# Page scatters of a mixture-of-experts kernel: each waits for the scatter two places ahead in its group of six

## The reference

```
h = silu(x @ eg_w[e].T) * (x @ eu_w[e].T)      # 128 -> 64
routed = sum over the 6 chosen e of weight_e * (h @ ed_w[e].T)
```

## Time and profile before

| | |
|---|---|
| median of 3 runs | 593.04 us (592.63 to 596.7) |
| span of the profiled execution | 792.4 us |
| mean granted TensorE clock in it | 0.675 |
| busy: PE, PE weight loads | 503.3 us, 420.8 us |
| busy: DVE, ACT, POOL | 456.1 us, 352.3 us, 389.3 us |
| stage 1 ends (first page load) | 379.52 us |
| first gather | 454.37 us |

### The profile page before, as it was taken

One profiled execution on the slowest core, in us unless ns is written; L12 is line 12 of the kernel. 1 busy time (PEld: TensorE's weight loads), 2 busy tenths in 40 slices (PEclk: granted clock), 3 DMA queues, 4 the chain that ended last, 5 costly groups with the idle time before them and its releaser, 6 DMA issues.

```text
span 792.4 us, 12061 instructions
## 1 busy us (share of the span) xinstructions
PE 503.3 (64%) x3204; PEld 420.8 (53%) x3204; DVE 456.1 (58%) x2264; ACT 352.3 (44%) x962; POOL 389.3 (49%) x425
## 2 busy tenths in 40 slices
PE   3767555766555574632359956788688889777700
PEld 2445334444334343311359856778688789777700
DVE  6587556667555576656233624576776756346532
ACT  3564433344443343322215934466666766246400
POOL 2006445654455655556650055454554545555574
PEclk9885555555555555555568976899988876897555
DMA  7532123322123332223425533455455555654421
GB/s 195 194 113 94 62 100 107 104 100 98 47 80 107 107 100 98 95 78 129 124 81 134 148 94 95 106 138 151 126 145 137 151 137 146 160 153 107 113 70 47
DMA packets 98708, 90.60 MB, mean 114 GB/s; under 512 B 10576, under 2 KB 85456, under 8 KB 98640
## 3 DMA queue, kind: packets, MB, share of 16 engines
q1 hardware_dynamic: 85232, 64.26, 27.5%
q0 software_dynamic: 12288, 25.29, 11.3%
q10 hardware_dynamic: 1120, 0.28, 0.2%
HBM read 41.32 MB, written 48.46 MB: 113 GB/s over the span
## 4 chain that ended last, share of the span: by engine, by line
PE 30%; another core or an unknown queue 17%; issue 16%; ACT 14%; POOL 11%; DVE 9%; ACTq 2%; DMA 0%; POOLq 0%; DVEq 0%
PE bank_s L1155 14%; POOL pages L447 6%; PE bank_o L1155 4%; PE bank_q L1155 3%; PE bank_s L1151 2%; ACT d_now L511 2%; ACT p_t L533 2%; ACT pxt L511 2%; POOL empty L492 2%; ACT gu_now L511 2%; ACT k_exp L521 1%; ACT s_act L672 1%; POOL p_t L492 1%; PE bank_o L1151 1%
## 5 line engine op out<-in xcount | busy, mean ns | idle before, releaser
L1155 PE MATMUL bank_s<-pxt,gu_now 128*128 128x64 f32 x768 | 116.5, 316 | 51.6 <-ACT pxt L511 31.3
L492 POOL DMA_INDIRECT p_t<-results,place_i x96 | 91.1, 949 | 110.6 <-ACT s_act L672 72.8
L1155 PEld LDWEIGHTS bank_s<-pxt,gu_now 128*128 128x128 f32 x768 | 111.4, 231 | 58.1 <-ACT pxt L511 36.4
L492 POOL DMA_INDIRECT empty<-results,place_i x96 | 91.1, 949 | 77.2 <-issue 35.1
L1111 DVE TENSOR_TENSOR h_t<-bank_s,s_act 64x256 f32<-64x256 f32 x128 | 54.7, 427 | 113.9 <-ACT s_act L672 95.4
L447 POOL DMA_INDIRECT pages<-payload,place_i x96 | 93.0, 968 | 37.9 <-issue 27.0
L447 POOL DMA_INDIRECT pages<-payload_b,place_i x96 | 92.8, 967 | 35.8 <-issue 26.7
L437 POOL TENSOR_TENSOR rstd<-ve,minus_half 128x4 f32<-128x4 f32 (+1 forms) x21 | 18.6, 885 | 132.6 <-DVE ve L927 130.0
L672 ACT ACTIVATE s_act<-bank_s 64x512 f32<-64x512 f32 x64 | 37.8, 590 | 79.5 <-remote 36.0
L533 ACT ACTIVATE p_t<-bank_s 128x512 f32<-128x512 f32 x64 | 36.2, 598 | 67.9 <-issue 27.9
L1255 PE MATMUL bank_o<-bias_h,row_h 96*128 96x256 bf16 x16 | 6.1, 381 | 72.2 <-ACT o_t L511 70.3
(11 more groups left out here) (169 smaller groups left out, 1164.1 us busy)
## 6 DMA issues: line engine op xcount, KB each, us to landing
pg<-pages SPq DMA_DIRECT2D x64, 258.0 KB
results<-y_s SPq DMA_DIRECT2D x64, 256.0 KB
pages<-empty SPq DMA_DIRECT2D x21, 774.0 KB
w_gu<-in_expert_gu SPq DMA_DIRECT2D x16, 256.0 KB
w_d<-in_expert_d SPq DMA_DIRECT2D x31, 128.0 KB
out_x<-xb SPq DMA_DIRECT2D x16, 128.0 KB
xb<-in_x SPq DMA_DIRECT2D x3, 512.0 KB, 8.0
pages<-payload,place_i POOLq DMA_INDIRECT x96
```

The lines of the kernel that those rows point to most:

```text
L492: pool.indirect_dma_start(out=ys[n % YS_SLOTS][:, k, :], out_offset=None, in_=results[0:landed * QUAD * P, :], in_offset=bass.IndirectOffs ...
L1155: return pe.matmul(dst, w, v, start=True, stop=True)
```

## The change

Each group of six scatters gets two semaphores in place of one, used in turn by even and odd k. From the third scatter of a group on, POOL waits before it issues scatter k until scatter k-2 has landed. The waits of SP, ACT and DVE for a whole group become two waits, each for half the count. Nothing else changes; data, rows and DMAs are the same.

```
--- before.py
+++ after.py
@@ -79,6 +79,7 @@
 UPFRONT = 5
 MADE = 8
 POWER_AFTER = {}
+IN_FLIGHT = 2
 
 
 def build(nc, x, ctx_cols, wq, bq, wk, bk, wv, bv, wo, bo, gate_cols, gate_bias, expert_gu, expert_d, shared_gu, shared_d, out, pages, results):
@@ -239,7 +240,7 @@
         logit_done, sig_ready, route, chosen_ready = sem("logit_done"), sem("sig_ready"), sem("route"), sem("chosen_ready")
         ranks_done, ranks_ready, placed = sem("ranks_done"), sem("ranks_ready"), sem("placed")
         payload_x, place_ready, digits_done, packed = sem("payload_x"), sem("place_ready"), sem("digits_done"), sem("packed")
-        scattered = [[sem(f"scattered{i}_{t}") for t in range(TPB)] for i in range(2)]
+        scattered = [[[sem(f"scattered{i}_{t}_{turn}") for turn in range(IN_FLIGHT)] for t in range(TPB)] for i in range(2)]
         page_in = [sem(f"page_in{j}") for j in range(SLOTS)]
         y_out = [sem(f"y_out{j}") for j in range(SLOTS)]
         pxt_done, pxt_ready, gu_done, act_ready, h_ready = sem("pxt_done"), sem("pxt_ready"), sem("gu_done"), sem("act_ready"), sem("h_ready")
@@ -363,7 +364,8 @@
             def pages_complete(batches):
                 for i in range(2):
                     for t in range(TPB):
-                        sp.wait_ge(scattered[i][t], 16 * TOPK * ((batches - i + 1) // 2))
+                        for landed in scattered[i][t]:
+                            sp.wait_ge(landed, 16 * TOPK // IN_FLIGHT * ((batches - i + 1) // 2))
 
             def store_results(q):
                 j = q % SLOTS
@@ -443,10 +445,13 @@
 
             def scatter(n, t, first, after):
                 wait_payload(n, t)
+                landed = scattered[n % 2][t]
                 for k in range(first, after):
+                    if k >= IN_FLIGHT:
+                        pool.wait_ge(landed[k % IN_FLIGHT], 16 * (TOPK // IN_FLIGHT * (n // 2) + k // IN_FLIGHT))
                     pool.indirect_dma_start(out=pages[:, :], out_offset=bass.IndirectOffsetOnAxis(
                         ap=place_i[:, TPB * n + t, k:k + 1], axis=0), in_=payload[n % 2][:, t, k, :],
-                        in_offset=None).then_inc(scattered[n % 2][t], 16)
+                        in_offset=None).then_inc(landed[k % IN_FLIGHT], 16)
 
 
 
@@ -578,7 +583,8 @@
 
             def fill_payload(n, side, t):
                 act.wait_ge(xn2_ready, TPB * n + t + 1)
-                act.wait_ge(scattered[n % 2][t], 16 * TOPK * (n // 2))
+                for landed in scattered[n % 2][t]:
+                    act.wait_ge(landed, 16 * TOPK // IN_FLIGHT * (n // 2))
                 copy(payload[n % 2][:, t, :, 0:D], xn2[side][:, t, :].unsqueeze(1).to_broadcast([P, TOPK, D])).then_inc(payload_x, 1)
 
             def body(b):
@@ -835,7 +841,8 @@
                 chained("filled_to", dve.tensor_tensor(filled_to[:, :], ranks[:, TPB, :], fill[:, :], ALU.add))
                 chained("rank", dve.tensor_tensor(rank[:, :, :], ranks[:, 0:TPB, :], both(fill), ALU.add))
                 for t in range(TPB):
-                    dve.wait_ge(scattered[n % 2][t], 16 * TOPK * (n // 2))
+                    for landed in scattered[n % 2][t]:
+                        dve.wait_ge(landed, 16 * TOPK // IN_FLIGHT * (n // 2))
                 chained("expert", dve.tensor_copy(pay[:, :, :, EXPERT].bitcast(U32), top_at[:, :, 8 - TOPK:8]))
                 after("filled_to")
                 chained("full", dve.tensor_scalar(full[:, :], filled_to[:, :], float(U), None, ALU.is_gt))
```

## The result

The changed kernel takes 646.68 us (643.7 to 647.64, four runs) beside 593.56 us for the kernel before on the same chip (592.63 to 596.7): 1.088 times as long, interval 1.0835 to 1.0921. It is slower, as forecast, but by 53 us where the forecast had 17, and it lies outside the range that I gave, 592 to 622 us.

What follows compares the result with a forecast made beforehand. POOL's own path was taken to bound timed runs, summing to 593 us without slack; 13 bodies delayed 1.4 us beside SP's burst make 18 us, taken as 17: 610 us, forecast's own range 602 to 618, whole range 592 to 622.

Steps and rivals of the forecast that it cites:

- POOL has no slack in a timed run: Stage 1: timed runs leave no room for an idle POOL, at most 0 to 0.7 us a body.
- The sum of POOL's path: Whole run: 290.5 us to first page load, then 12.1 + 43 + 238 + 9.1, in all 593 us, the median.
- The rival in which the slack swallows the waits: Stage 1: POOL's idle time absorbs the 1.4 us a body, so 593 to 597 us; chance 0.27.
- a quiet wait is free: Scatters outside SP's burst: packets started 2.1 us after issue, 0.4 us before scatter k wants to start; no cost.
- the 2.15 us that the prediction set beside them: Quiet scatter of 66 KB: the Trainium skill's estimate, about 2.0 us plus bytes / 436 GB/s; no quiet scatter waits.
- the size of a landing beside the burst: t = 1 groups: fourth scatter lands 3.6 us after issue, sixth starts 1.4 us later; 13 x 1.4 = 18 us.
- the delay is one and not a sum of several: t = 1 groups: the fifth scatter's wait is part of the sixth's 1.4 us delay, not one more.
- More than one wait in a group: Rival: with 0.78 us releases quiet groups wait too, 13 x 2.7 = 35 us, 628 us; 0.14 with lower clock.
- The lower clock: Rival: longer POOL bodies idle PE to half clock, 626 us for five bodies, 680 for all; 0.14 shared.
- the sign that the prediction gave: If quiet groups wait as well, the wrongly sized term is the release, from landing to scatter's start, 0.28 or 0.78 us.
- Nothing became faster: Rival: fewer POOL packets beside SP's burst let it land sooner, 585 us or only 0.6 us gained; chance 0.05.
- some 20 us less of waiting for `ve`: Sign in the changed trace: POOL's wait for DVE's `ve` falls from 130.0 us by some 20 us, if half clock again.

Runs made afterwards that it cites:

- the added instruction: The kernel before with one more small POOL instruction per body, between `rstd` and the t = 1 scatters, its result unused: 610.91 us, 1.026 times before.

## Why the prediction was right in its direction and wrong in its size

**That POOL has no slack in a timed run: right.** The sum of POOL's path made 593 us, and the slack was put at 0 to 0.7 us a body. The trace without waits has its terms: first page load at 294.8 (290.5 in the sum), 51 us from there to the first gather (55), 242 us to the last gather (238), 9.1 to the end (9.1), 596.8 in all. Each is within 5 us, so the sum did not come out by luck. The slack is 0.2, by the added instruction, and the loss reaches the end whole (48 us at the first page load, at the first gather and at the end). The rival in which the slack swallows the waits, with 0.27, is refuted, and so is its basis, the 7.3 us of idle time in the trace of before.

**Why that trace showed them: my reading was wrong, and it didn't enter the sum.** I saw TensorE at half clock there and took the timed runs to have the full one. The body of the kernel without waits runs at the same clock, 0.50, with the same PE work, in 16.54 us (columns as in the earlier trace rows):

```profile
106.07:122.61 16.54, 14.00 (x84) 9.56 (x80) 14.46 (x87) 9.19 (x23) 12.62 (x14) 0.50 0.38 130
```

Most of the 7 us lay on ACT. Before, then without waits, ACT's `sig`, which waits for PE's four matmuls over `gw_t`:

```profile
102.17 1.11 PE L1155 MATMUL bank_r<-gw_t,x_all 128*128 128x64 f32 x4
...
110.23 0.28 ACT L546 ACTIVATE sig<-bank_r 128x128 f32<-128x128 f32 x1 [3.68 <-remote]
```

```profile
97.02 1.12 PE L1162 MATMUL bank_r<-gw_t,x_all 128*128 128x64 f32 x4
...
98.71 0.31 ACT L551 ACTIVATE sig<-bank_r 128x128 f32<-128x128 f32 x1
```

In the profiled execution of before ACT stood idle for the 3.68 us up to 110.23, though PE had been done since 103.3, and once more for 2.60 us before `q_t`. In the trace without waits it is nothing and 0.96 us. What held ACT up in that execution stays open.

**That a quiet wait is free: wrong, by 0.6 us a group.** I took the landing at 2.1 us from the packets. It is 2.27 to 2.39 us, and 2.54 to 2.66 with the start, just over the 2.52 us that were free, and now and then a landing is 0.8 to 1.4 us later, likely by an instruction fetch. The 2.1 us were the time until all packets had started, and the landing came 0.4 us after that; the 2.15 us that the prediction set beside them were short as well. With 14 groups that is the 8.7 us of the run with waits at t = 0.

**The step that failed: the size of a landing beside the burst.** The forecast had 13 x 1.4 = 18 us here, and it was 39.0 us, 14 x 2.8. I read the landing from the number of packets that POOL's queue had started: 131 by 103.42 us, so the fourth scatter's 32 were through the earlier trace rows. The changed trace lets one do both readings for the same scatter, the third of its group, issued at 117.43. The queue from 114.38 us, when the group begins, to 121.00 us:

```profile
q1 hardware_dynamic: 445, 1.31, 58.4%
q0 software_dynamic: 97, 0.23, 9.5%
q14 instruction: 2, 0.02, 1.3%
```

97 packets are those of three scatters, so by my method it had landed 3.6 us after its issue. But the fifth scatter, which waits for it, starts at 122.42, 0.27 us after the landing: 4.7 us after the issue. A count says how many packets have started. It does not say whose they are, nor when they land. A scatter raises its semaphore 16 times, and by the times of these events in the trace the third's came from 121.15 to 122.15, while the fourth's began at 121.57, before the last four of the third. So some parts of the fourth scatter landed before the last ones of the third. What held those up, SP's packets (58.4% of the DMA engines' time) or the 8 KB fetch that ran here from 120.68 for 0.83 us, this one scatter does not show. The semaphore is full only with the last part, and even in quiet 0.4 us after the last packet has started: of the scatter at 124.94 and the one before it, all 64 packets had started at 126.90, and the landing is at 127.34.

```profile
q0 software_dynamic: 64, 0.13, 20.9%
```

It is not this scatter alone. In the run with waits at t = 1 alone, the third scatters of all 14 such groups land 4.6 us after their issue on average (3.1 to 6.0), and the count of packets gives 3.5 for the same ones. Their first packets set out only 2.7 us after the issue, in place of 1.5 in quiet.

With the landing measured, the same working gives the right size: 4.7 + 0.27 - 2.52 = 2.4 us at the fifth scatter, beside the 2.8 measured with a small part at the others, and 14 x (2.4 + 0.6) = 42 us of 47.5; the average landing of 4.6 us gives the same to 0.1 us a body. That the delay is one and not a sum of several was right: half the waits cost 41.9 of 47.5 us. And the pair that counts is the third and fifth, and in two of the 14 bodies the fourth and sixth; I had looked at the second pair alone.

**The rivals.** "More than one wait in a group", with 0.14 together with the lower clock, had the quiet groups waiting too, but at too small a price, 35 us, and for a reason that does not hold: the release takes 0.27 us and not 0.78. So the sign that the prediction gave, "the release is the term that I sized wrongly", points at the wrong term; it is the landing. The lower clock was no cause: stage 1 runs mostly at it with and without waits (mean 0.54 in both traces, from the first scatter to the first page load). Nothing became faster.

**What would have shown it.** I had expected some 20 us less of waiting for `ve` and idle times up to 1.5 us; the wait fell by 87 us, all of it the disturbance (without waits it is 42.9 us, with them 43.1), and idle times go to 2.7 us.

## What to carry to other kernels

A wait on a DMA costs the time to the last of its 16 parts, not to its average packet: take it from the landing of a semaphore, and where the trace has none, as a lower bound only. Beside other traffic it was up to three times the quiet value (7.3 us against 2.3), so a margin of 0.4 us, as I had reckoned from started packets, is none. And before a wait goes on an engine that seems to have idle time, add up that engine's own work against the measured time of the runs: here the sum was right and the idle time in the profile was not that of the timed runs.

## What the runs showed of the hardware that I had not expected

- From the last started packet of a scatter to its landing it was 0.4 us in quiet (126.90 to 127.34), and from the landing to the start of the waiting DMA 0.27 us, the same in the changed kernel and with one in flight.
- One scatter, the sixth of (9, t = 0), started 1.61 us after its release in six traces, whatever the traffic. No run shows why.
- Scatters of 66 KB beside a burst of 1.3 MB from SP landed up to 5.2 us after their issue in the changed kernel and 7.3 us in the one with three in flight. With all loads first, the one issued at 108.72 took 7.4 us. The issue of a scatter took POOL 0.95 to 1.08 us all the same, the very first aside.
- A single instruction fetch packet of 16 KB, 1.06 us on one DMA engine, went with a landing 1.5 us later than in quiet (3.8 in place of 2.3). That it was the cause is not shown.
